# Twenty-four attention units in one stream: stacks loaded ahead of the rows of maxima, a split of q on VectorE, and new orders of work

## The reference

```python
# layer 0
s = einsum(q, k) / sqrt(8) + slope[h] * (j - i)      # self attention, band of 64 keys, per-head slopes
x = layernorm(x + softmax(where(band, s, -1e9)) @ v @ wo + bo)
x = layernorm(x + mha(x, mem))                        # cross attention over 512 keys
x = layernorm(x + gelu(x @ w1 + b1) @ w2 + b2)
# layer 1
q = rmsnorm(x, g_q) @ Wq; k, v = rmsnorm(mem, g_c) @ Wk, Wv
out = rmsnorm(x + softmax(q k / sqrt(8)) v @ Wo, g_out)
```

## Time and profile before

| | us |
|---|---|
| median of 3 runs | 572.91 (572.53 to 574.24) |
| the profiled execution, its own time | 571.68 |
| its span on the core | 569.9 |
| busy in the span: TensorE, VectorE, ScalarE, GpSimd | 506.6, 442.7, 427.1, 338.8 |

### The profile page before, as it was taken

One profiled execution on the slowest core, in us unless ns is written; L12 is line 12 of the kernel. 1 busy time (PEld: TensorE's weight loads), 2 busy tenths in 40 slices (PEclk: granted clock), 3 DMA queues, 4 the chain that ended last, 5 costly groups with the idle time before them and its releaser, 6 DMA issues.

```text
span 569.9 us, 17389 instructions
## 1 busy us (share of the span) xinstructions
PE 506.6 (89%) x6772; PEld 276.4 (49%) x6772; DVE 442.7 (78%) x911; ACT 427.1 (75%) x658; POOL 338.8 (59%) x640
## 2 busy tenths in 40 slices
PE   3577879877789999999999999999999999998984
PEld 2345556654434444455554545454545454444432
DVE  6335555646989999888889898989888999999912
ACT  3136666645367888989898989898898888787793
POOL 7344488883549627566576767675858384663032
PEclk9969999989989999999999999999999999999998
DMA  3957655564616347060615162425435361524000
GB/s 104 214 118 211 180 155 158 154 189 102 167 54 141 116 74 185 9 183 20 169 55 134 50 141 87 104 87 102 127 64 138 62 177 52 152 91 89 3 21 19
DMA packets 90195, 63.51 MB, mean 111 GB/s; under 512 B 6446, under 2 KB 89630, under 8 KB 90026
## 3 DMA queue, kind: packets, MB, share of 16 engines
q1 hardware_dynamic: 89540, 61.91, 42.0%
q10 hardware_dynamic: 574, 0.49, 0.5%
HBM read 34.99 MB, written 26.22 MB: 107 GB/s over the span
## 4 chain that ended last, share of the span: by engine, by line
PE 62%; DVE 8%; SPq 8%; ACT 7%; issue 6%; DMA 5%; POOL 4%; ACTq 0%; POOLq 0%; DVEq 0%
PE pv L646 20%; PE ps L627 11%; PE ps L582 10%; DVE negmax L945 6%; ACT probs L781 5%; PE ps L692 3%; PE ps L744 3%; PE ps L681 3%; PE ps L708 3%; DMA kst<-k_parts 2%; SPq L441 2%; PE ps L671 2%; PE ps L732 2%; SPq L466 2%; DMA qst<-mT 2%
## 5 line engine op out<-in xcount | busy, mean ns | idle before, releaser
L945 DVE TENSOR_REDUCE negmax<-ps 128x1 f32<-128x512 f32 x512 | 320.5, 683 | 25.7 <-PE ps L627 20.3
L781 ACT ACTIVATE probs<-ps 128x1024 f32<-128x1024 f32 x288 | 287.5, 1025 | 67.5 <-PE ps L582 40.5
L646 PE MATMUL pv<-probs,vp 128*32 128x256 f32 (+1 forms) x3072 | 158.6, 334 | 2.8 <-issue 2.8
L627 PE MATMUL ps<-kst,qst 61*128 61x512 bf16 x512 | 104.9, 385 | 8.5 <-DVE negmax L945 5.4
L582 PE MATMUL ps<-qst,kst 64*128 64x256 bf16 x1024 | 97.5, 273 | 6.5 <-ACT probs L781 3.1
L646 PEld LDWEIGHTS pv<-probs,vp 128*32 128x32 f32 x3072 | 70.4, 111 | 54.9 <-issue 28.1
L1056 POOL TENSOR_SCALAR mcap<-negmax 128x16 f32<-128x16 f32 x48 | 12.2, 254 | 107.4 <-DVE negmax L945 43.7
L582 PEld LDWEIGHTS ps<-qst,kst 64*128 64x128 bf16 x1024 | 38.7, 94 | 63.0 <-issue 21.8
L941 DVE TENSOR_REDUCE negmax<-ps 128x4 f32<-128x512 f32 x64 | 40.2, 684 | 27.5 <-PE ps L618 27.5
L627 PEld LDWEIGHTS ps<-kst,qst 61*128 61x128 bf16 x512 | 27.5, 93 | 58.9 <-DVE negmax L945 31.4
L1093 POOL TENSOR_TENSOR qr<-qf,qs 128x256 f32<-128x256 f32 x24 | 16.1, 670 | 58.2 <-ACT qs L805 31.3
(11 more groups left out here) (132 smaller groups left out, 762.8 us busy)
## 6 DMA issues: line engine op xcount, KB each, us to landing
kst<-k_parts SPq DMA_DIRECT2D x64, 192.0 KB, 4.3
qst<-q_parts SPq DMA_DIRECT2D x48, 192.0 KB, 3.8
k_parts<-ks SPq DMA_DIRECT2D x16, 384.0 KB, 2.7
q_parts<-qs SPq DMA_DIRECT2D x24, 192.0 KB, 2.2
cin<-in_ctx_dram SPq DMA_DIRECT2D x16, 256.0 KB, 3.0
k_parts<-ks SPq DMA_DIRECT2D x16, 256.0 KB, 3.1
q_parts<-qs SPq DMA_DIRECT2D x24, 128.0 KB, 2.3
k_parts<-ks SPq DMA_DIRECT2D x24, 128.0 KB, 3.2
```

The lines of the kernel that those rows point to most:

```text
L627: mm = nc.tensor.matmul(empty_banks("X", u.index, n + g), q[rows_in(g, 0, ROW_M), four, tile * P:(tile + 1) * P], k[rows_in(g, 0, ROW_M), ...
L646: mm = nc.tensor.matmul(pv[32 * j:32 * j + 32, dst:dst + n], vp[u.parity][:, c, 4 * quad + j, :], probs[:, quad, src:src + n], start=(quad ...
L781: nc.scalar.activation(to, src, ACT.Exp, scale=SCALE).then_inc(act_emptied, 1)
L945: ins = nc.vector.tensor_reduce(negmax[:, tile, at:at + 1], src, AX.X, ALU.max, negate=True)
```

## The change

All texts of the order are new, with other sequences and other banks. A new item R stands behind Q where unit i+2 is a self unit: VectorE makes the three subtractions of q (`part_q`), and GpSimd's `split` for q runs only for units of the later stages. `load_stacks` comes ahead of M0's rows in every step. The first loads of stacks 0 to 2 wait for the zeroing of the stack, not for its constant rows; the rows of stacks 1 and 2 are both copied from ScalarE's queue, ahead of the first V. Loads of constants and later weights move from the head of step 0 to the end of step -1. VectorE lays out the later weights at the head of step 2 instead of at B. The context of a sequence is loaded at the end of its own step and its squares (C) are taken one step later.

```diff
-SELF = "C B3 XC:56 V:0 raw Q:3 S:45 M1:1 D:0 K:1 X:43 S:56 X:21 P0 X:04 S:23 P1 A:5 M0:0 S:34 X:51 O:2 P2"
+SELF = "XC:56 B3 Q:0 M1:2 R K:5 raw X:34 X:60 S:12 V:5 X:43 S:12 S:56 P0 D:4 P1 M0:2 X:65 C A:4 S:23 P2 O:0"
...
-FIRST_SELF = ("XC:01 B3 raw V:1 Q:4 S:01 M1:5 X:32 K:1 S:12 X:30 X:26 D:5 A:5 S:45 P0 S:12 M0:6 C X:53 P1 B:5 P2 "
+FIRST_SELF = ("B3 XC:45 raw Q:0 K:4 S:12 M1:3 R S:34 X:50 V:2 P0 X:56 B:0 X:52 D:5 P1 A:4 S:34 X:56 O:5 S:12 M0:0 "
...
-NEXT_SELF = "XC:34 Q:5 K:0 M1:6 S:12 B3 S:34 raw X:52 X:40 P0 C D:4 M0:6 X:15 P1 V:0 X:61 S:45 S:01 A:4 O:1 P2"
+NEXT_SELF = "XC:45 B3 Q:4 K:1 M1:6 raw C X:52 S:12 X:56 X:23 V:1 X:26 D:5 S:01 A:0 R M0:6 S:01 P0 P1 S:34 O:2 P2"
...
-CROSS_FFN = ("S:01 X:56 XC:23 X:45 S:01 B3 S:23 X:64 Q:1 S:56 X:03 K:2 raw X:41 X:03 M1:6 H:52 D:0 P0a X:61 P0b "
+CROSS_FFN = ("XC:45 S:12 X:36 B3 S:34 X:01 S:56 X:04 S:23 Q:1 raw X:50 K:6 X:34 X:25 H:01 X:43 P0a X:42 M1:0 S:56 "
+             "D:3 P0b S:12 X:40 S:56 sq F:3 S:56 X:40 S:12 V:3 P1a S:45 S:01 X:63 M0:2 P1b X:45 X:36 S:12 P2a S:45 "
+             "X:01 S:23 P2b A:6 X:43 S:01 S:56 X:24 P3a T:0 O:1")
...
             elif name == "C":
-                yield "context", self.main, None, at
+                yield "context", self.before if 0 < self.i <= B else None, None, at
+            elif name == "R":
+                yield "split", self.n if self.n is not None and self.n.stage == 0 else None, None, at
...
                 if n.index < STACKS:
-                    sp.wait_ge(stack_rows[n.stack], STACK_ROWS[n.stack])
+                    sp.wait_ge(stack_zeroed[n.stack], 2)
...
-                if s.i == -1:
-                    sp.wait_ge(ones_loaded, 64)
-                    sp.wait_ge(stack_zeroed[1], 2)
-                    copy_rows(sp, 1)
-
-                early = s.i < 0 or s.i >= B
-                if s.n is not None and early:
+                if s.n is not None:
                     load_stacks(s.n)
                 if s.nxt is not None:
                     load_maxima(s.nxt, 0)
-                if s.n is not None and not early:
-                    load_stacks(s.n)
+                if s.i == -1:
+                    sp.dma_start(cols[:, :], a["columns"]).then_inc(cols_loaded, 16)
+                    for dst, src in const_loads():
+                        sp.dma_start(dst, src).then_inc(consts_loaded, 16)
+                    sp.dma_start(win[:, 3:9, :], a["w_in"][:, 3:9, :]).then_inc(win_rest, 16)
+                if s.main is not None and s.main.stage == 0:
+                    load_early(s.main.batch)
...
+            def part_q(u):
+                dve.wait_ge(act_emptied, ACT_AT["Q", u.index] + 1)
+                nc.vector.tensor_tensor(qr[:, :], qf[:, :], qs[:, 0, :], ALU.subtract).then_inc(q_steps, 1)
+                nc.vector.tensor_tensor(qs[:, 1, :], qf[:, :], qs[:, 0, :], ALU.subtract).then_inc(q_steps, 1)
+                dve.wait_ge(q_steps, 3 * u.index + 2)
+                nc.vector.tensor_tensor(qs[:, 2, :], qr[:, :], qs[:, 1, :], ALU.subtract).then_inc(q_steps, 1)
...
                 if s.n is not None:
-                    split(s.n, qf, qr, qs, LQ, "Q", q_steps)
+                    if s.n.stage > 0:
+                        split(s.n, qf, qr, qs, LQ, "Q", q_steps)
                     split(s.n, kf, kr, ks, KEYS[s.n.stage], "K", k_steps)
```

58 lines of the change are left out of this document (27 added, 31 removed).

## The result

| | before | after |
|---|---|---|
| median of four runs, us | 572.72 (571.04 to 574.24) | 585.92 (582.76 to 587.21) |
| ratio | | 1.0223, interval 1.0173 to 1.0273 |
| profiled execution, its own time and its span | 571.68, 569.9 | 582.76, 580.7 |
| busy: TensorE, VectorE, ScalarE, GpSimd | 506.6, 442.7, 427.1, 338.8 | 514.1, 451.8, 427.4, 323.8 |

The changed kernel is 2.2% slower; the forecast was 1.1% faster. The profiled execution of after is the fastest of its four, so the spans differ by 10.8 us and the medians by 13.2. GpSimd lost 15 us, the cuts of q, and VectorE, which makes them now, has 9 more.

The account below looks back on a forecast made before the run. Self steps were taken as bound by latency, cross steps by nearly full engines, step 7 by VectorE. 571.68 - 2.8 - 3.75 - 3.0 + 3.6 = 565.7; from the median 566.9, forecast 566.5 us, range 559.5 to 572.

Parts of the forecast that it names:

- The regimes: Self steps bound by latency, cross and feed-forward steps by nearly full engines where only order counts, step 7 by VectorE.
- The start: Up to step 1: earlier stack loads, K ahead of the first S and a shorter wait at B gain 2.8 us, bounds 0.5 and 5.
- the wait ahead of B: At the start: TensorE's 2.14 us wait for weights on VectorE goes, of which 0.8 us was counted as gained.
- R's 0.42: VectorE's three subtractions of q: 0.42 us each, 1.3 in all, with 0.3 and 0.67 as bounds.
- The self steps: Steady self steps fall from 13.05 to 12.3 us, GpSimd next to bind at 12.0: 3.75 gained, bounds 0 and 5.3.
- the wait ahead of X for the stacks: Self steps: TensorE's wait ahead of X for the DMA of `kst` was to be gone.
- The second rival: Self steps: late M0's rows or R and k's cuts blocking each other use up the 3.75; 570.5 us, chance 0.17.
- Steps 6 to 8: Forecast for steps 6 and 7: VectorE's long series begins 18.6 to 18.9 us behind XC; 3.0 gained, bounds 1 and 4.
- Feed-forward steps: Steps 11 to 18: 27.8 us instead of 27.36, 3.6 lost in all; bounds 0.2 gained and 1.0 lost a step.
- The line through gelu: Feed-forward step: ScalarE's work to the first exponential behind gelu ends at 13.2 us, then TensorE needs 14.55.
- Plain cross steps: Cross steps without feed-forward: 23.2 to 23.4 us as now, no change, bounds 0.3 either way for each of seven.
- The third: Rival: new banks in fifteen cross steps lose 12.2 us against 9.6 gained, so slower at 575.5; chance 0.13.

Follow-up runs that it names:

- before_queue: The kernel before with the stack loads issued ahead of M0's rows in the self steps too: 588.6 us, 1.0284 of before.
- the best mixture: Changed kernel, old feed-forward, plain and last cross texts; C, w1/w2 loads, B moved; q of units 0, 1 on GpSimd; stack 2's rows copied later: 563.2 us, 0.9857.

## Why the prediction was wrong, point by point

**What bounds the kernel.** The regimes were right for the self steps (latency) and the cross steps (order). That the cross steps could only cost or save a little was right in each and wrong in the sum, since there are sixteen of them.

**The start, 2.8 gained: nothing found** (XC of step 1 at 48.8 in the mean of the ten profiles with the start and R as changed, between 46.5 and 51.0, and 48.80 before). The first S came at 33.58, where I had 31.9 and before has 33.28. Two steps failed. The loads of stack 1 did not come sooner, since the eight issues on ScalarE's queue, for which I had written that ScalarE has nothing else to do, slowed SyncE's issues of the stores that the loads wait for (6.38 against 3.88 us; the loads began at 27.96, before at 26.41). And the wait ahead of B did not go: the bias columns stand behind the reductions of X:56 on VectorE, and I had looked only at what no longer stands ahead of them. The first X came 2.6 later, not 1.6. R's 0.42 was right where GpSimd was not in its way (0.35 to 0.43); its third operation took 0.78 or 0.93 in three of the eight steps.

**The self steps, 12.3 each: 12.72,** 1.7 us gained instead of 3.75 by the mean, 1.3 by the two profiles, and neither is clear of the spread. The bound was misnamed: SyncE's loop over two landings, not GpSimd. The wait ahead of X for the stacks, which I had as gone, is there as before (3.4 us in steps 1 to 5, 2.7 before). The second rival named a mechanism, M0's rows holding the first score: it makes 1.3 us of waits in these five steps of after and none before, but 15.0 in before_queue, the queue order without its text.

**Steps 6 to 8, 3.0 gained: 1.6 lost** from XC of step 6 to the first tile of step 9 (70.5 us instead of 68.9): 1.9 lost in step 6, 0.2 gained in 7 and 8. SyncE's part of the walk held: k's loads of unit 8 went out 13.0 us behind XC (125.60), where I had 13.2. The step that failed is TensorE's, which I had at its X 16.1 behind XC. It came there at 23.15:

```profile
135.71 0.39 PE L620 MATMUL ps<-kst,qst 61*128 61x512 bf16 x1
```

Ahead of that it had stood for 1.48, 2.38, 1.12, 0.44 and 1.94 us in step 6. The second is C's: I had walked this step on TensorE, SyncE and VectorE, not on ScalarE, where C had moved ahead of the first exponential and its load behind M0's rows. Both moves were in the diff; I had charged C only at step 8. The last has no cause that the profile shows. So VectorE's long series began at 136.14, 23.6 behind XC, instead of 18.6 to 18.9.

**Feed-forward steps, +0.45 each: +0.66,** and 6.3 in all instead of 3.6, with 1.2 of it the wait of step 16 for M0's rows, which I had left out. The line through gelu was there (13.5 and 14.55 us, forecast 13.2 and 14.55), yet only half of the loss hangs on it: without the tables the new text still loses 0.34 to the old. That the forecast for a step came so near is in part luck: the walk had waits of 2 us in a new step and over 1 in an old one, and the rows have 0.78 and 0.43.

**Plain cross steps, nothing: +0.5 each (steps 9 and 20), 0.7 in step 10,** which leads into the feed-forward steps, and 3.2 from step 19 to the end. My bound was 0.3 a step. TensorE waits 4.3 us behind XC of step 20, after, for a reduction:

```profile
485.95 0.39 PE L620 MATMUL ps<-kst,qst 61*128 61x512 bf16 x2 [0.32 <-DVE negmax L944]
```

and before, from XC of step 9 to XC of step 10, it waited over 0.1 us for one only at the end:

```profile
207.53 0.39 PE L627 MATMUL ps<-kst,qst 61*128 61x512 bf16 x1 [0.26 <-DVE negmax L945]
```

Reductions are in the chain of step 20 of both kernels (8.3% of it after, 8.9% before), so that VectorE is in the path is not new. The new text has more such waits and 0.16 us more of busy time; which of its moves makes them, no run takes apart.

**The rivals.** The third was the right one in kind: the new texts lose from step 9 on. It gave 575.5, 10 below what came, since it kept the 9.6 of gains ahead of step 9, of which the profile has none. The two errors were of like size: 9.7 us of gains that did not come, and 10.7 of losses where I had put 3.6. The range, 559.5 to 572, was too narrow at the upper end because it took the gains as independent of each other, though all of them pass through steps 6 to 8, and gave the cross texts bounds that the new order broke.

## What to carry to other kernels

An order of work and the order of a DMA queue are one design: test them together and apart, since here each alone costs over 3 us a step and both together cost nothing. Price a new wait of TensorE with the clock that it may lose: about half of those 3 us was more busy time at the lower clock. Walk every engine through a rewritten step, also those that are not full: an item of 1.6 us ahead of the one exponential that frees a bank made TensorE wait 2.4. And take a change of many texts apart by text: some of its parts were worth keeping and others not, and the best mixture is 1.4% faster than before where the whole was 2.2% slower.
